# All steps of a fused conv + FFN kernel written out instead of looped, and square roots with a constant epsilon

## The reference, cut to what matters

```
n = (x - mean_c) / sqrt(var_c + 1e-6)          # over the 96 channels
x = x + (depthwise_conv3x3(n) + n)
t = (x - mean_c) / sqrt(var_c + 1e-5)          # over the 96 channels
h = relu(q(t8 @ W1_8.T) + b1_8)                # 384 hidden units; _8: rounded to fp8 e5m2
y = q(h8 @ W2_8.T) + b2_8                      # q: rounded to fp16
out = x + y
```

## Time and profile before

| | |
|---|---|
| runs | 3359.96, 3360.18, 3365.55 us |
| median | 3360.18 us |
| profiled execution, its own time | 3365.72 us |
| its span | 3364.0 us |
| busy share of the span: DVE / ACT / PE / POOL | 95% / 93% / 90% / 57% |
| HBM traffic | 539.84 MB read, 168.59 MB written |

### The profile page before, as it was taken

The page is one execution under the profiler, slowest core; times in us unless marked ns, Lnnn a source line. Parts: engine busy times, 40 slices in busy tenths (PEclk is TensorE's granted clock), DMA queues, the critical chain, the costliest instruction groups (busy, mean ns, idle before and its releaser), DMA issues.

```text
span 3364.0 us, 87592 instructions
## 1 busy us (share of the span) xinstructions
PE 3014.8 (90%) x24902; PEld 2505.1 (74%) x24902; DVE 3211.1 (95%) x11767; ACT 3142.8 (93%) x7072; POOL 1921.2 (57%) x915
## 2 busy tenths in 40 slices
PE   5689999899998999989999899989999999999877
PEld 5577777777777777777777777777777777778744
DVE  8559999999999999999999999999999999999998
ACT  7779999999999999999999999999999999987776
POOL 0005666556665666656666566656666666666676
PEclk9999999999999999999999999999999999999966
DMA  6777777777776777777777777767777777776533
GB/s 219 213 201 216 225 225 225 216 223 222 224 224 206 224 227 228 223 208 226 223 222 225 208 225 225 229 203 226 224 224 222 225 229 223 225 201 183 157 120 99
DMA packets 277528, 714.48 MB, mean 212 GB/s; under 512 B 35001, under 2 KB 35106, under 8 KB 277026
## 3 DMA queue, kind: packets, MB, share of 16 engines
q1 hardware_dynamic: 271394, 694.12, 70.5%
q10 hardware_dynamic: 5632, 14.45, 1.3%
HBM read 539.84 MB, written 168.59 MB: 211 GB/s over the span
## 4 chain that ended last, share of the span: by engine, by line
DVE 66%; issue 14%; PE 9%; ACT 8%; DMA 2%; DVEq 1%; SPq 0%; ACTq 0%; POOL 0%; POOLq 0%
DVE stats L654 22%; DVE xq L691 19%; DVE hid L644 10%; PE conv_ps L434 6%; DVE hid L649 5%; DVE images L703 5%; ACT images L526 3%; ACT hid L505 3%; DVE xt_ps L678 2%; PE hid_ps L397 1%; DVE rstd L682 1%; DVE neg_mean L686 1%; DVEq L183 1%; PE y_ps L412 1%; DVE y L671 1%
## 5 line engine op out<-in xcount | busy, mean ns | idle before, releaser
L434 PE MATMUL conv_ps<-images,band_ring 112*112 112x222 f32 (+1 forms) x8928 | 1884.4, 356 | 29.8 <-DMA band_ring<-bands 29.5
L434 PEld LDWEIGHTS conv_ps<-images,band_ring 112*112 112x112 f32 x8928 | 1553.2, 178 | 180.5 <-issue 31.9
L279 POOL TENSOR_TENSOR xf<-xf,y 112x768 f32<-112x768 f32 x448 | 952.0, 2125 | 1174.3 <-DVE y L671 1174.3
L505 ACT ACTIVATE hid<-hid_ps 128x896 f16<-128x896 f32 x1344 | 1191.9, 928 | 91.6 <-PE hid_ps L397 88.3
L274 POOL TENSOR_TENSOR xf<-xf,images 112x768 f32<-112x768 f32 x448 | 981.4, 2191 | 264.4 <-ACT images L537 246.7
L526 ACT ACTIVATE images<-xn,neg_mean,rstd 112x96 f32<-112x96 f32 x2590 | 1044.5, 556 | 21.3 <-DVE neg_mean L686 16.8
L412 PEld LDWEIGHTS y_ps<-w2t,hid 128*128 128x128 f16 x10752 | 576.4, 100 | 410.7 <-ACT hid L505 221.6
L412 PE MATMUL y_ps<-w2t,hid 128*128 128x96 f16 x10752 | 672.9, 210 | 210.8 <-ACT hid L505 186.9
L691 DVE SCALAR_TENSOR_TENSOR xq<-xf,stats,xt_ps 112x96 fp8e5<-112x96 f32 x3584 | 843.7, 317 | 0.0
L397 PE MATMUL hid_ps<-xt,w1t 96*128 96x448 fp8e5 x2688 | 684.1, 364 | 24.0 <-ACT xt L497 24.0
L644 DVE TENSOR_SCALAR hid<-hid,b1q 128x896 f16<-128x896 f16 x1344 | 594.6, 473 | 16.4 <-ACT hid L505 15.3
(11 more groups left out here) (55 smaller groups left out, 824.6 us busy)
## 6 DMA issues: line engine op xcount, KB each, us to landing
band_ring<-bands SPq DMA_DIRECT2D x744, 294.0 KB, 5.1
xf<-in_x SPq DMA_DIRECT2D x462, 336.0 KB, 5.0
out<-xf SPq DMA_DIRECT2D x448, 336.0 KB, 3.8
xn<-in_x SPq DMA_DIRECT2D x434, 336.0 KB, 3.4
bands<-images ACTq DMA_DIRECT2D x16, 882.0 KB, 8.0
xf<-bands SPq DMA_DIRECT2D x24, 294.0 KB, 4.4
xf<-in_L_ffn_W SPq DMA_DIRECT2D x2, 144.0 KB, 3.1
xf<-in_L_conv_kernel SPq DMA_DIRECT2D x3, 3.4 KB
```

Of the source, the lines that this page charges most:

```text
L279: pool.tensor_tensor(res, res, y[:, e % 2], ALU.add).then_inc(summed, CW)
L434: mm = pe.matmul(dst[:, :, lo:hi], band_place(t < CONV_AT + UNIT, n)[:, PAIR * dx + i, :], images[:, m % 2, :, ch, lo + dx - 1:hi + dx - 1 ...
L505: nc.scalar.activation(hid[:, e % 2, TOK * j:TOK * (j + 1)].rearrange("p (u n) -> p u n", u=2), hid_ps[:, k, :, 0:HALF * H], ACT.Identity) ...
```

## The change

`LAST` becomes 0, so `run` never opens the loop: the steps 5 to 450 are all written out with r = 0, and every wait value and address is a constant. The epsilon of the square roots becomes a constant of the instruction; the tile `eps` and the two fills by POOL are gone, and the counts on the semaphore `consts` are lower by one.

```
-        eps = sb("eps", [H, 2], F32)
...
-        LAST = max(0, (TOTAL - LOOP - 4 - LOOP_AT) // LOOP)
+        LAST = 0
...
-                for i, v in enumerate((EPS_T, EPS_C)):
-                    op = pool.memset(eps[:, i:i + 1], v)
-                op.then_inc(consts, 1)
...
-                pool.wait_ge(consts, 5)
+                pool.wait_ge(consts, 4)
...
-                pe.wait_ge(consts, 14)
+                pe.wait_ge(consts, 13)
...
                 def root_t(r, e):
                     wait(act, stats_t_done, LOOP * r + e + 1)
                     nc.scalar.activation(std[:, e % 2, 0, :], stats[:, e % 2, 0, :, 2], ACT.Sqrt,
-                                         bias=eps[:, 0:1], scale=1.0 / C).then_inc(std_t_done, 1)
+                                         bias=EPS_T, scale=1.0 / C).then_inc(std_t_done, 1)
                 def root_c(r, n):
                     wait(act, stats_c_done, LOOP * r + n + 1)
                     nc.scalar.activation(std[:, n % 2, 1, :], stats[:, n % 2, 1, :, 2], ACT.Sqrt,
-                                         bias=eps[:, 1:2], scale=1.0 / C).then_inc(std_c_done, 1)
+                                         bias=EPS_C, scale=1.0 / C).then_inc(std_c_done, 1)
...
-                dve.wait_ge(consts, 14)
+                dve.wait_ge(consts, 13)
```

More of the change, by code:

```diff
@@ L251, in _ @@
                 pool.memset(taps_16, 0.0).then_inc(consts, 1)
-                pool.wait_ge(consts, 5)
+                pool.wait_ge(consts, 4)
                 for k, rows in enumerate(part_rows):
                     if k:
-                        pool.wait_ge(consts, 5 + 2 * k)
+                        pool.wait_ge(consts, 4 + 2 * k)
                     pool.affine_select(out=shift[rows, :], in_=ones[rows, :], pattern=[[1, 2 * H]],
@@ L261, in _ @@
                                        channel_multiplier=-1).then_inc(consts, 1)
-                pool.wait_ge(consts, 11)
+                pool.wait_ge(consts, 10)
                 pool.affine_select(out=ident[:, :], in_=ident[:, :], pattern=[[1, P]], compare_op=ALU.is_equal,
```

## The result

The changed kernel takes 3324.75 us in the median of 4 runs (3322.81 to 3330.84), the kernel before 3360.07 (4 runs, 3355.07 to 3365.55). The ratio is 0.9896, with a 95% interval from 0.9882 to 0.9909: 1.0% faster. 3327 was forecast. The profiled execution took 3330.84 us, 34.9 less than the profiled one before.

What follows compares the result with a forecast made beforehand. DVE was taken to bound full steps at 6.93 us, with five loop returns adding time. Returns -32.6 and roots -2.0 gave 3325.6 us from the median or 3331.1 from the profiled execution; 3327 was taken, range 3319 to 3336.

Steps and rivals of the forecast that it cites:

- The five returns: Loop going back to its start, 395 us apart: removing all five was to save 32.6 us.
- the five excesses: Time over 6.93 us a step at each place where the loop goes back: 5.8 to 6.9 us, 32.6 together.
- the lower bound: At the returns, only TensorE's halts go, slow products stay: about 22 us saved; as a rival 3336 us, chance 0.04.
- the slow products: TensorE's 12 convolution products after a halt: 3.99 and 4.55 us against 2.31 elsewhere, expected to go with the halts.
- Constant waits in 336 steps: Fewer sequencer instructions on every engine in the loop's steps, hidden under DVE's full occupation: 0.
- boundaries of 28 chunks: In full steps, DVE about 0.4 us late; gain taken as 0, up to 5 us in the ACT's relief rival, chance 0.07.
- Straight code: Written-out code instead of a body used six times; instruction fetches were to cost DVE no idle time: 0.
- the rival of late blocks: Instruction blocks arriving late in the straight code, about 2 us each; with one in six late, 3430 us; chance 0.04.
- The roots: ACT's square roots with constant epsilon, 23 on the start-up chain: 0.09 us saved each, 2.0 us in all.
- My straight line through two wider shapes: ACT's L481 and L537 extrapolated to 8 columns: 143 ns for a root that takes 292.
- The 5.5 us between the profiled execution and the median: Profiled execution's excess over the median: in untouched places gives 3325.6 us, in the five returns 3331.1; 3327 taken.

Runs made afterwards that it cites:

- ACT alone: Changed kernel with the loop of six passes put back on ACT only, other engines written out: 3337.6 us, one run.
- all but PE: Changed kernel with the loop of six passes on every engine except TensorE, whose steps are written out: 3341.3 us, ratio 0.9937 to the kernel before.
- second run: The full change measured again, unaltered, beside the written-out kernel that keeps the tile eps: 3326.05 us, ratio 0.9894 to the kernel before.
- direct comparison: Full change against the same written-out kernel with roots still reading the tile eps, side by side on one chip: 3326.05 against 3327.85 us.
- the roots alone: Changed kernel with the loop put back, so only the constant epsilon differs from the kernel before: 3355.5 us against 3361.2, ratio 0.9986.
- TensorE alone: Changed kernel with the loop of six passes on TensorE only, other engines written out: 3352.2 us, ratio 0.9968 to the kernel before.

## Why the prediction was right

**The five returns, -32.6 us.** Right in size and cause. In the profiled executions the five excesses are gone to 0.1 us. The halts alone would have been 22 us, the lower bound that I kept; they did not go alone: the slow products went with them. Where TensorE doesn't loop, the clock stays at 1.00 at most returns. It falls to 0.95 in a window of 34 us at one return of ACT alone (the second) and at one of all but PE (the third, against what I expected). These two alone have a further 0.8 us of excess in the next step, and the excess of each is the largest of its run's five. TensorE had then stood for ACT's L493, 2.3 and 1.8 us, so the clock can fall after a wait as after a halt of TensorE's own. At the second return of all but PE it stood 2.2 us and the clock stayed at 1.00: what makes the difference is open.

**Constant waits in 336 steps, 0.** The full step is 6.93 us in all of these kernels. It was argued from DVE's full occupation and stays so. One small thing I had not split off: the boundaries of 28 chunks are 0.3 us over a step in the changed kernel and were 0.4 before, 1.0 us over eight. It isn't shown that the constants did this. The second run of the same changed kernel shows 0.3 to 0.5 at these places again, so I leave it as a difference between executions.

**Straight code, 0, and the rival of late blocks.** 203 + 206 packets of instructions in the whole span, fewer than the 219 + 283 before, and no idle time of DVE marked "issue" in full steps. The rival fell.

**The roots, -2.0 us.** The size of one saving, taken at 0.09 us, is 292 - 200 = 92 ns, and the 93 ns that the Trainium skill gives for a pointer operand (ScalarE: Activation LUTs, What ACT_TABLE_LOAD costs) agree. My straight line through two wider shapes had given a saving of 149 ns, too much. Their worth in the whole is 1.8 us in the direct comparison (ranges overlap), 5.7 with the loop in place, 1.2 on the chain by 107 us. I read that as about 2; the runs don't fix it better.

**The 5.5 us between the profiled execution and the median.** I left open where they lie and split the difference. They can lie in the start-up, which varies by as much. L678 (now L674) from 236 to 270 us before and after, and from 236 to 262 us in the second run of the changed kernel:

```profile
L678 DVE RECIPROCAL xt_ps<-std x4: 192/204/211, 243.4 to 265.5; 112x8 f32<-112x8 f32 x4
```

```profile
L674 DVE RECIPROCAL xt_ps<-std x4: 195/204/211, 240.5 to 265.0; 112x8 f32<-112x8 f32 x4
```

```profile
L674 DVE RECIPROCAL xt_ps<-std x4: 204/208/211, 238.8 to 257.9; 112x8 f32<-112x8 f32 x4
```

The fourth start is at 265.5 before, at 265.0 after and at 257.9 in the second run. The last two are 7.1 us apart, and the two executions of the changed kernel took 3330.84 and 3323.70, 7.1 apart too. No profile of a 3360 us execution of the kernel before was taken, so for that kernel it stays likely and not shown. The profiled execution after had gained 2.9 us by its first start and lost 2.4 of them again by the fourth: POOL waits there for the loads of `xf` (4.7 us the longest, 5.9 before). So the transfers of the first chunks decide a few us of any execution, and the roots' gain can vanish in them. Taken rightly, the sum would have been 3360.2 - 34.6 = 3325.6; 3324.75 was measured.

## What to carry to other kernels

A hardware loop whose body is long costs at every return, not at every step: look for the period of the loop in the starts of one line that runs once a step, and compare the return with the loop's last pass, which goes on without one. Price it by what the bounding engine loses, which is more than its own halt when another engine in its chain halts longer. How far back the return goes matters: POOL's pass of 236 recorded instructions brought no halt. If a loop must stay, write out the engine with the longest halt first: together with the new roots, that brought 3362.6 to 3341.3 us here.

## What the runs showed of the hardware that was not expected

TensorE mostly halts longer at a far return (2.9 to 4.9 us) than ACT (2.1 to 4.0) or DVE (1.3 to 2.2). Why is open. The queue q8 is TensorE's: it moves 219 packets when TensorE loops and 203 when only the others do. Its packets are twice the size of q14's (3.33 MB / 203 = 16 KB against 1.69 MB / 206 = 8 KB), but no run here varied that.

The halt is not constant. With the roots alone the third and the fourth return of one execution read, on its chain:

```profile
1450.03 4.86 issue
1455.44 4.55 PE conv_ps L430 x12
...
1846.12 2.88 issue
1849.55 3.80 PE conv_ps L430 x12
```

A halt of 4.86 us is followed by 12 products in 4.55 us, one of 2.88 by 3.80, where 2.31 is the time at the full clock: 2.2 us lost against 1.5. But the loss doesn't simply grow with the halt. With TensorE alone, the first and the fifth return read:

```profile
660.28 3.36 issue
664.19 4.55 PE conv_ps L430 x12
...
2242.21 3.46 issue
2246.03 3.99 PE conv_ps L430 x12
```

Halts of 3.36 and 3.46 us lose 2.2 and 1.7 us, and the 4.18 us of the earlier trace rows lose 1.7. What differs is the time at 1.2 GHz: the granted clock is 0.50 from 662.3 to 669.1 us at the first of these two returns, and only from 2246.1 to 2249.5 at the other. Why it is longer at one is open.
